# Twelve-stage decoder: initial loads split between the program's start and the first stage, int8 operands prepared one stage earlier

## What is computed

```python
x = _layernorm(x + _L0_attn_ref(x, ...), axis=-1)
...
x = _layernorm(x + _L2_xattn_ref(x, ctx_1024, ...), axis=-1)
x = _layernorm(x + _L2_ffn_ref(x, L2_ffn_rhs), axis=-1)
...
```

```python
def _absmax_scale(x, axes):
    amax = jnp.max(jnp.abs(x), axis=axes, keepdims=True)
    return jnp.maximum(amax, 1e-12) / INT8_MAX
lhs_scale = _absmax_scale(lhs, (2,))
rhs_scale = _absmax_scale(rhs, (0,))
q_lhs = jnp.clip(jnp.round(lhs / lhs_scale), -INT8_MAX, INT8_MAX).astype(jnp.int8)
q_rhs = jnp.clip(jnp.round(rhs / rhs_scale), -INT8_MAX, INT8_MAX).astype(jnp.int8)
```

## Time and profile before

| | us |
|---|---|
| median of 3 runs | 3002.65 |
| lowest and highest of them | 3000.22 and 3006.18 |
| profiled execution | 2984.8 |
| its span, first to last instruction | 2982.8 |

### The profile page before, as it was taken

One profiled execution on the slowest core, in us unless ns is written; L12 is line 12 of the kernel. 1 busy time (PEld: TensorE's weight loads), 2 busy tenths in 40 slices (PEclk: granted clock), 3 DMA queues, 4 the chain that ended last, 5 costly groups with the idle time before them and its releaser, 6 DMA issues. The chain is left out here.

```text
span 2982.8 us, 51441 instructions
## 1 busy us (share of the span) xinstructions
PE 2786.1 (93%) x20384; PEld 1798.5 (60%) x20384; DVE 1915.4 (64%) x3469; ACT 1223.0 (41%) x2596; POOL 363.1 (12%) x483
## 2 busy tenths in 40 slices
PE   6999999999998978999999989999898999989898
PEld 3666466666666868566666667766564333346576
DVE  4676377777764347577777743356567999966532
ACT  1333354445542345455444421143242866633211
POOL 1111000000002710000000000022211000001232
PEclk9999999999999989999999999999999999999999
DMA  3001100000012331100000000100000000000341
GB/s 128 14 14 40 75 10 5 5 5 5 5 68 77 95 130 37 43 5 6 9 5 5 37 18 1 34 21 18 22 18 32 19 1 1 1 18 19 106 168 67
DMA packets 43244, 103.54 MB, mean 35 GB/s; under 512 B 4929, under 2 KB 32687, under 8 KB 39425
## 3 DMA queue, kind: packets, MB, share of 16 engines
q1 hardware_dynamic: 37217, 86.66, 8.2%
q0 software_dynamic: 5792, 13.59, 1.5%
HBM read 66.74 MB, written 19.07 MB: 29 GB/s over the span
## 5 line engine op out<-in xcount | busy, mean ns | idle before, releaser
L2586 ACT ACTIVATE prob<-R,neg_max 128x333 f32<-128x333 f32 x512 | 268.4, 537 | 184.2 <-DVE neg_max L2655 183.9
L4135 DVE TENSOR_TENSOR_SCAN arena<-arena,u 128x512 f32<-128x512 f32 x256 | 289.6, 1204 | 0.1
L2474 PEld LDWEIGHTS T<-const,prob 128*128 128x128 f32 (+1 forms) x1536 | 184.0, 144 | 81.9 <-DVE prob L2668 36.7
L2668 DVE TENSOR_TENSOR prob<-prob,rec 128x666 f32<-128x666 f32 x256 | 218.4, 853 | 19.5 <-issue 0.4
L2655 DVE TENSOR_REDUCE neg_max<-R 128x2 f32<-128x666 f32 x256 | 205.9, 846 | 35.2 <-PE R L2463 35.2
L2474 PE MATMUL T<-const,prob 128*128 128x128 f32 (+1 forms) x1536 | 211.4, 274 | 13.0 <-DVE prob L2668 10.7
L2593 ACT ACTIVATE prob_t<-T 128x384 f32<-128x384 f32 x256 | 125.5, 490 | 228.8 <-PE T L2474 222.7
L4066 ACT ACTIVATE arena<-delta,neg_a 128x510 f32<-128x510 f32 x256 | 175.6, 714 | 43.8 <-DVE arena L4135 42.9
L2661 DVE COPY prob_t<-T 128x384 f32<-128x384 f32 x256 | 142.3, 556 | 40.1 <-PE T L2474 15.1
L2393 PE MATMUL O<-keys_in,arena 128*128 128x333 f32 x512 | 164.9, 444 | 0.0
L3969 PE MATMUL R<-arena,diag 64*64 64x512 f32 x1024 | 136.0, 621 | 24.3 <-DVE arena L4135 24.2
(11 more groups left out here) (610 smaller groups left out, 5403.6 us busy)
## 6 DMA issues: line engine op xcount, KB each, us to landing
w<-w_dram SPq DMA_DIRECT2D x16, 1024.0 KB, 7.0
arena<-pack_dram SPq DMA_DIRECT2D x2, 4100.0 KB, 15.2
q_pad<-q_pad SPq DMA_DIRECT2D x24, 224.0 KB, 2.7
arena<-pack_dram SPq DMA_DIRECT2D x4, 1284.0 KB, 6.8
arena<-pack_dram SPq DMA_DIRECT2D x1, 4896.0 KB, 14.7
slots_in<-x_nat SPq DMA_DIRECT2D x2, 2048.0 KB, 9.5
arena<-planes SPq DMA_DIRECT2D x8, 512.0 KB, 8.2
arena<-k_nat SPq DMA_DIRECT2D x16, 224.0 KB, 2.7
```

The lines of the kernel that those rows point to most:

```text
L2474: last = nc.tensor.transpose(S.T[0:n, i, kc * P:(kc + 1) * P], prob[:, g % 2, i, first:first + n], S.ident)
L2586: last = nc.scalar.activation(prob[:, g % 2, i, :], S.R[:, g % 2, i * BANK:i * BANK + XK], ACT.Exp, bias=neg_max[:, g % 2, i:i + 1], accum ...
L2668: nc.vector.tensor_tensor(prob[:, g % 2, :, :], prob[:, g % 2, :, :], rec[:, g % 2, :].unsqueeze(2).to_broadcast([P, 2, XK]), ALU.mult)\
L4135: nc.vector.tensor_tensor_scan(state[:, q % HELD, :], decay[:, q % DEEP, :], u[:, i % 2, :], 0.0, ALU.mult, ALU.add)\
```

## The change

**Loads.** The first block now loads only the first two batches' columns of x_t and the three matrices write1, write2 and read (`LINE_COLS`). Everything else is issued by SP at the head of the first stage: the rest of the pack in two parts, const, the context tiles, the rest of x_t, x_nat and ctx_t. The waits move accordingly: the engines wait for `weights_ready` to reach 32 only where they first need the rest, ACT behind its first copy; the mask casts move into the first stage; `x_ready` now counts three loads. The buffers filled are the same.

**Int8.** Stage 7 is told that the int8 stage follows (`int8=True`). DVE quantises the columns there at i = 1 and the rows of batches 0 and 1 at i = 7 and 8; TensorE turns them at i = 8, 9 and 10 and ACT copies them out. The int8 stage then starts with the product of batch 0, and its loop on DVE begins at batch 2. Its buffers lie in the arena behind the pack, instead of in tensors of the stage. The six `keep_warm` matmuls of the int8 stage and one in stage 7 are gone.

```diff
+FIRST_BATCHES = 2
+LINE_COLS = slice(PACK[0]["write1"][0], sum(PACK[0]["read"]))
+OTHER_COLS = [slice(0, LINE_COLS.start), slice(LINE_COLS.stop, sum(n for _, n in PACK[0].values()))]
...
+def later_loads(nc, S, sp):
+    first = FIRST_BATCHES * T
+    for t, n in CTX_TILES:
+        sp.dma_start(context_rows(S)[t][0:n, :], S.ctx_dram[t * P:t * P + n, :]).then_inc(S.marks.c_in, 16)
+    sp.dma_start(S.x_t[:, :, first:N], S.xt_dram[:, :, first:N]).then_inc(S.x_ready, 16)
+    sp.dma_start(S.x_nat[:], S.x_dram).then_inc(S.x_ready, 16)
+    sp.dma_start(S.ctx_t[:], S.ctxt_dram).then_inc(S.x_ready, 16)
...
+Int8 = namedtuple("Int8", "rhs_i rhs_q rows_i rows_q col_scale col_inv unround row_scale row_inv")
+EARLY_ROWS = 2
...
+def int8_columns(nc, S, dve, I, k):
+    rhs = part(S.arena[k % 2], PACK[k], "rhs_t", C)
+    dve.wait_ge(S.weights_ready[k], 16)
+    nc.vector.memset(I.unround, -ROUND)
+    int8_scale(nc, dve, rhs, I.col_scale, I.col_inv)
+    int8_rounded(nc, I.rhs_i, rhs, I.col_inv)
+    dve.drain()
+    int8_bounded(nc, I.rhs_i)
+    dve.drain()
+    for nb in range(C):
+        last = nc.vector.tensor_scalar(I.rhs_i[:, nb, :], I.rhs_i[:, nb, :], ROUND, I.col_scale[:, nb:nb + 1], ALU.subtract, ALU.mult)
+    return last
...
+def int8_rows(nc, S, dve, I, b):
+    x = S.x_nat[:, b * TT:(b + 1) * TT, :]
+    int8_scale(nc, dve, x, I.row_scale[:, b % 4, :], I.row_inv)
+    int8_rounded(nc, I.rows_i[:, b % 2, :, :], x, I.row_inv)
+    dve.drain()
+    return int8_bounded(nc, I.rows_i[:, b % 2, :, :])
...
+            def columns_turned():
+                settle(pe, M.setup_bc, 1)
...
+            def rows_turned(b):
+                pe.wait_ge(M.exp_done, 2 * B)
+                pe.wait_ge(M.diff_sb, b + 1)
...
                     pe.wait_ge(M.neg_sb, B)
-                    keep_warm(nc, S, S_q, 1)
+                    if int8:
+                        columns_turned()
+                    else:
+                        keep_warm(nc, S, S_q, 1)
+                if int8 and 0 <= i - B - 1 < EARLY_ROWS:
+                    rows_turned(i - B - 1)
...
+                if int8 and i == 1:
+                    int8_columns(nc, S, dve, I, k + 1).then_inc(M.setup_bc, 1)
                 if 0 <= i - 2 < B:
                     quotient(i - 2)
+                if int8 and i == B - 1:
+                    int8_rows(nc, S, dve, I, 0).then_inc(M.diff_sb, 1)
                 if 0 <= i - 3 < B - 1:
                     residual(i - 3)
+                if int8 and i == B:
+                    int8_rows(nc, S, dve, I, 1).then_inc(M.diff_sb, 1)
...
+            for cols in OTHER_COLS:
+                geometry_weights(nc, S, sp, cols).then_inc(S.weights_ready[k], 16)
+            sp.dma_start(S.const[:], S.const_dram).then_inc(S.const_in, 16)
+            later_loads(nc, S, sp)
             sp.wait_ge(M.pads, 1)
...
+                    if i == -AHEAD and tt == 0:
+                        pe.wait_ge(S.weights_ready[k], 32)
...
-                        pe.wait_ge(S.x_ready, 32)
+                        pe.wait_ge(S.x_ready, 48)
...
+                if i == -AHEAD:
+                    act.wait_ge(S.weights_ready[k], 32)
+                    nc.scalar.activation(lam[:], part(W, TB, "decay"), ACT.Exp, scale=-1.0)
+                    nc.scalar.activation(lam_rows[:], part(W, TB, "decay_rows"), ACT.Exp, scale=-1.0).then_inc(M.lam_exp, 1)
+                    act.wait_ge(M.setup, 1)
...
-            dve.wait_ge(S.weights_ready[k], 16)
-            nc.vector.tensor_scalar(bq_s[:], part(W, TB, "bq"), scale, None, ALU.mult).then_inc(M.setup, 1)
...
+            nc.vector.memset(cmv[:], 1.0)
+            dve.wait_ge(S.weights_ready[k], 32)
+            nc.vector.tensor_scalar(bq_s[:], part(W, TB, "bq"), scale, None, ALU.mult).then_inc(M.setup, 1)
...
+            settle(dve, S.const_in, 16)
+            masks_cast(nc, S)
...
+            pool.wait_ge(S.weights_ready[k], 32)
+            pool.wait_ge(S.x_ready, 48)
...
             unread = S.R[:, 0, BANK:2 * BANK]
-            rows(0)
-            keep_warm(nc, S, unread, 6)
-            settle(pe, M.setup, 1)
-            for kc in range(C):
-                for nb in range(C):
-                    last = nc.tensor.transpose(S.O[:, 0, kc * D + nb * P:kc * D + (nb + 1) * P], rhs_i[:, nb, kc * P:(kc + 1) * P], S.ident)
-            last.then_inc(M.k_full, 1)
-            settle(pe, M.k_sb, 1)
             for i in range(B + 3):
                 if i < B:
                     product(i)
                 if i + 1 < B:
-                    rows(i + 1)
+                    if i + 1 >= E:
+                        rows(i + 1)
                     keep_warm(nc, S, unread, 1)
...
-            nc.vector.memset(unround[:], -ROUND)
-            for i in range(B + 3):
+            for i in range(E, B + 3):
...
-                sp.dma_start(S.x_t[:], dram["x_t"].rearrange("(c p) n -> p c n", p=P)).then_inc(loaded, 16)
-                sp.dma_start(S.const[:], dram["const"]).then_inc(loaded, 16)
-                prefetch(nc, S, sp, layers[0])
-                sp.dma_start(S.x_nat[:], dram["x"].rearrange("(t p) d -> p t d", p=P)).then_inc(S.x_ready, 16)
+                first = FIRST_BATCHES * T
+                sp.dma_start(S.x_t[:, :, 0:first], S.xt_dram[:, :, 0:first]).then_inc(loaded, 16)
                 if layers[0] == 0:
-                    for t, n in CTX_TILES:
-                        sp.dma_start(context_rows(S)[t][0:n, :], S.ctx_dram[t * P:t * P + n, :]).then_inc(S.marks.c_in, 16)
-                sp.dma_start(S.ctx_t[:], dram["ctx_t"].rearrange("(c p) n -> p c n", p=P)).then_inc(S.x_ready, 16)
+                    geometry_weights(nc, S, sp, LINE_COLS).then_inc(loaded, 16)
+                else:
+                    prefetch(nc, S, sp, layers[0])
+                    sp.dma_start(S.const[:], S.const_dram).then_inc(loaded, 16)
+                    later_loads(nc, S, sp)
...
-            lambda k: cross16(nc, S, k, DH16 ** -0.5, k == layers[0]),
+            lambda k: cross16(nc, S, k, DH16 ** -0.5, k == layers[0], int8=True),
```

More of the change, by code:

```diff
@@ L488, in _ @@
                     product(i - 1, 0)
[L489 removed]
+            keep_warm(nc, S, bank(0), 2)
+            if int8:
+                settle(pe, M.diff_sb, EARLY_ROWS)
+                settle(pe, M.odd_sb, 1 + EARLY_ROWS)
             settle(pe, M.k_sb, 2 * C)
```

147 lines of the change are left out of this document (80 added, 67 removed).

## The result

The changed kernel takes 2989.8 us (median of five, 2986.7 to 2993.1), the kernel before 3006.2 (3000.2 to 3012.1). The ratio is 0.9951, 95% interval 0.9937 to 0.9965: **14.7 us less, between 10.5 and 19** (the two medians lie 16.4 us apart). I had forecast 16.7 less and 2986.0, with 2979 to 2994 as range.

A forecast was written before the change was run, and what follows sets the result against it. TensorE is busy 93% of the span, so only places where it idles count: 6.9 us at the first stage's start plus 9.8 at the int8 head make 16.7, from the timed median 3002.65 to 2986.0; range 2979 to 2994.

The forecast's parts named there:

- The start of the stage: First stage: TensorE starts at 6.5 instead of 20.0, 13.5 us earlier, since SP's own queue had held it.
- rival 4: First stage starts no earlier because something other than SP held it; only 9.8 us gained, 2992.9; chance 0.06.
- Inside the stage: First stage: GpSimd's chain behind the last loads sets the first feature transposes, at 35.0 instead of 43.8, 8.8 us earlier.
- rival 2: First stage: loads slower, ctx_t 4 us later at 32, GpSimd's chain moves fully; 12.7 us less, 2990.0; chance 0.14.
- The clock: First stage: TensorE restarts at 1.2 GHz after its new wait, making the chain behind it 1.9 us longer.
- rival 1: First stage: TensorE keeps 2.4 GHz through its new wait; 18.6 us less, 2984.1; chance 0.15.
- Rival 5: From the first stage on: TensorE stays at 1.2 GHz after its new wait, kernel slower, 3010; chance 0.03.
- part 1: First stage, new loads: transposes 8.8 us earlier less 1.9 for the clock, worth 6.9 us.
- The int8 head: Int8 stage: first products start with the stage, VectorE's first result at 2267.5 instead of 2278.74, 11.2 us less.
- The end of cross attention: Cross attention's end: VectorE's inserted rows and TensorE's turning cost 1.4 us together, bounds 0 and 5.4.
- Rival 3: Cross attention's end: VectorE's insertions cost their full 5.4 us; 12.7 us less in all, 2990.0; chance 0.13.
- The condition I had set for being wrong: Whole kernel: wrong if untouched stages change over a microsecond or two, or anything but GpSimd's chain sets the first transposes.

The follow-up runs named there:

- loads alone: Only the new loads put into the kernel before, with cross attention and the int8 stage as before: ratio 0.9982 to the kernel before, 5.4 us less.
- rows earlier: Changed kernel with both batches' rows quantised on VectorE two rounds earlier in cross attention: ratio 0.9949 to the kernel before.
- those with four and with eight warming matmuls: Changed kernel with four or eight warming matmuls instead of two in TensorE's first-stage wait for GpSimd: ratios 0.9953 and 0.9964 to the kernel before.

## Why the prediction was right

**The start of the stage.** Forecast 6.5, measured 7.63. SP's queue was the holder, as said (rival 4 is out: 12.4 us earlier). The 1.1 us are the first microseconds of transfer: 10, 199, 254, 363, 387 GB/s where the earlier trace rows had 66, 147, 393, 393, 442, and the pack's piece landed at 7.2. I had carried over the rates of one 2 MB load to one of 512 KB with one of 768 KB behind it.

**Inside the stage.** Every link was the forecast one, each a little late: ScalarE's second copy 15.29 (13.5), last line copy 22.29 (20.5), VectorE's context done and unit lines begun 24.55 (24.0), GpSimd released by ctx_t 30.07 (28.4), feature transposes 36.34 (35.0). I had read their place before one row too early: 43.80 is a weight load, and the first of the matmuls comes behind the warming ones (timeline of before):

```profile
44.22 0.60 PE L1707 MATMUL T<-const,arena 128*112 128x128 f32 x4
```

So they are 7.9 us earlier. Of rival 2 a part was true: loads about 1.6 us later than summed, not 4. That GpSimd's chain sets the transposes is shown, since changing its order alone moved them by 2.7 us.

**The clock.** The direction was right and rival 1 is out: TensorE fell back after its 3.78 us of waiting, and warming matmuls removed the low stretch. The charge of 1.9 us is the mean of five executions (7.7 against 5.8 us, 1.2 to 2.4 in single ones). That it fits to the tenth is luck: I had put the low level at 4 us, and it lasted 3.4 in two of the five and 6.8 to 13.7, in part ahead of the transposes, in the others. The Trainium skill (TensorE: Matmul & The Clock Gate, "What's actually happening") has activity release the throttled state, and both the low stretch behind the wait and its absence behind the shorter one agree. Rival 5 is out: the clock was back by 41.7. The next line matmuls were due at 43.1 by my sum (35.0+6.2+1.9). They came at 43.39 in the first profile, 6.6 us earlier than before (49.99), and at 44.1 in the mean of the five, against 49.9 in the mean of the four profiles with the loads of before: 5.8 us. So what failed of part 1 is the arrival of the loads, not the clock. The rest of the stage has a further low stretch near 60 us in some executions of both kernels. Compared like with like, the second stage begins at 360.0 with the loads of before against 354.5 (mean of two profiles and of three) where the stretch is there, and at 357.8 against 352.5 (two and two) where it isn't: 5.5 and 5.4 us. So **5.4 of the 6.9** remain; where the last 0.4 goes was not looked for. The profiles with the smaller gain (loads alone, rows earlier) had low stretches of 6.8 to 13.7 us between 28 and 42 us, where after had 3.4.

**The int8 head.** 11.2 us in seven of the nine profiles with both batches, and 10.9 in the other two (those with four and with eight warming matmuls). The step was exact because a later instruction's wait was replaced by the product's own duration, and both stood in rows.

**The end of cross attention.** 1.4 us forecast. It was made up of 0.9 for the last reciprocal and 0.4 for TensorE's turning, which is 1.3; measured in the profile of after are 1.4 and 0.3, together 1.7. The picture is right: no idle time is left before the reciprocal, and two operations beside GpSimd's adds take 1.0 us more, where I had 0.8. The Trainium skill (SBUF — State Buffer, "Who interferes with whom") has full exclusion, by which I had estimated up to 1.3; the trace shows a little less. But this step was incomplete. With the rows at that late place, four of seven profiles had the further low stretch near 110, and the reciprocal 3.7 to 4.6 us late. The mean over the seven is 3.1 us, against 0.3 over the four without any insertion: some 2.7, and with the turning 3.0, not 1.4. With so few executions this is rough. Moving the insertions into idle time took the 2.7 away (0.1 late at the short stretch, and 1.5 at the long one, where the loads alone have 1.6) and left the 0.3. So the term that was missing is the clock: I had priced VectorE's delay, but not that the wait it gives TensorE can lower the clock for 6.8 us more. Rival 3, which put 5.4 us there, came near in half the executions, by the clock and not by VectorE's full durations.

**The sum.** 5.4 + 11.2 - 3.0 = 13.6 from the profiles, 13.7 and 14.7 from the timings, 16.7 forecast. The excess of 3.1 us is in the first stage (1.5) and the tail (1.6), and the range held it. The choice to start from the timed median and not from the profiled time, 18 us lower, was needed, but I had no reason for the 18 us: the profile of before shows the short third stage (169.2 us), and its timed runs presumably had the long one. A forecast from the profiled time, 2968.1, would have missed by 22 us. The condition I had set for being wrong, untouched stages that change by more than a microsecond or two, was met by that stage in the first pair of profiles. It was a poor sign to choose: the same stage lasts 169.1 in the second profile of the changed kernel.

## What to carry to other kernels

When early loads are split, the next holder is whoever waits for *all* of them: look on each engine's queue for work that stands behind the joint wait without needing it (here GpSimd's features, 2.7 us). Insert extra work in a round where the engine idles, not in the last rounds where its delay makes TensorE wait: beside the direct delay, such a wait can cost the clock. A charge for the clock varies between executions of one kernel (1.2 to 2.4 us here), so look at several profiles before you call its size right or wrong. And compare profiles stage by stage, since one untouched stage can move by more than the change is worth.

## What the hardware showed that I had not expected

- The third stage, fed by gathered and scattered rows, ran in 169 or in 190 to 196 us, by session and with the same instructions, bytes and busy time of its transfers (about 55 us in both lengths); the cause is open.
- A low clock stretch near the same place of a stage lasted 3.4 us in one execution and 6.8 in the next, and moved the stage's end by 1.6 us with unchanged code (loads alone against before).
- TensorE fell to 1.2 GHz in or behind waits of 2.8 to 4.3 us in the first stage, in seven profiles of seven, and did not after 1.47 us there. In cross attention it fell after waits of 2.6 and 2.9 us, and in two of the four profiles with a wait of 1.2 us, all four of which had a low stretch that ended some 6 us before it.
